# Three groups of single-column products behind the shared expert's tiles, in a four-layer kernel on one core

## The reference

```
sh = gelu(xt @ sw1 + sb1) @ sw2 + sb2
sh = sh + gelu(xt @ swd) @ swu
out = out + 0.2 * sh
```

```
xk = x * time_mix_k + (1.0 - time_mix_k) * xx
xv = x * time_mix_v + (1.0 - time_mix_v) * xx
xr = x * time_mix_r + (1.0 - time_mix_r) * xx
k = jnp.einsum('btc,oc->bto', xk, w_key)
v = jnp.einsum('btc,oc->bto', xv, w_value)
r = jax.nn.sigmoid(jnp.einsum('btc,oc->bto', xr, w_rec))
...
ww = time_first + k
```

## Time and profile before

| | us |
|---|---|
| median of 3 runs without a profile | 866.83 (865.06 to 867.51) |
| profiled execution | 858.83 |
| its span, first to last instruction | 856.3 |
| TensorE busy in it | 838.8 (98%) |

### The profile page before, as it was taken

One profiled execution on the slowest core, in us unless ns is written; L12 is line 12 of the kernel. 1 busy time (PEld: TensorE's weight loads), 2 busy tenths in 40 slices (PEclk: granted clock), 3 DMA queues, 4 the chain that ended last, 5 costly groups with the idle time before them and its releaser, 6 DMA issues.

```text
span 856.3 us, 15659 instructions
## 1 busy us (share of the span) xinstructions
PE 838.8 (98%) x5436; PEld 710.0 (83%) x5436; DVE 631.1 (74%) x1275; ACT 472.1 (55%) x944; POOL 455.6 (53%) x316
## 2 busy tenths in 40 slices
PE   8999999999999999999999999999999999999998
PEld 7888888888856899999999878778888887886688
DVE  6899999999987756655656969577667695345767
ACT  3666666676654566646643375633453425357743
POOL 6676767676614655666666021059718216708720
PEclk9999999999999999999999999999999999999999
DMA  8101010101007275456113050011111010030001
GB/s 335 39 20 37 18 37 18 37 18 37 0 1 273 87 255 202 151 185 206 63 44 96 40 209 1 0 51 50 37 37 37 13 62 1 1 148 3 3 2 50
DMA packets 23342, 62.17 MB, mean 73 GB/s; under 512 B 3136, under 2 KB 13632, under 8 KB 20224
## 3 DMA queue, kind: packets, MB, share of 16 engines
q1 hardware_dynamic: 21760, 57.35, 19.5%
q0 software_dynamic: 1536, 4.20, 1.5%
HBM read 50.00 MB, written 8.39 MB: 68 GB/s over the span
## 4 chain that ended last, share of the span: by engine, by line
PE 85%; DVE 8%; ACT 2%; POOL 2%; issue 1%; DMA 1%; SPq 0%; DVEq 0%; ACTq 0%; POOLq 0%
PE banks L102 25%; PE banks L104 24%; PE banks L103 24%; PE banks L1344 3%; DVE banks L1875 1%; PE banks L1330 1%; POOL arenaB L841 1%; POOL arenaC L841 1%; DVE arenaC_rounded L1884 1%; PE banks L999 1%; PE banks L1171 1%; PE banks L934 1%; PE banks L933 1%; PE banks L1013 1%; PE banks L854 1%
## 5 line engine op out<-in xcount | busy, mean ns | idle before, releaser
L2079 ACT ACTIVATE banks<-banks,small 128x512 f32<-128x512 f32 x128 | 84.9, 663 | 74.2 <-DVE small L1480 74.2
L1480 DVE TENSOR_REDUCE small<-banks 128x1 f32<-128x512 f32 x128 | 87.1, 680 | 4.9 <-PE banks L104 4.9
L104 PE MATMUL banks<-arenaC_rounded,arenaD_rounded 128*128 128x512 f32 (+1 forms) x256 | 89.4, 349 | 0.0
L102 PE MATMUL banks<-xnT_rounded,arenaD_rounded 128*128 128x512 f32 x224 | 88.1, 393 | 1.3 <-POOL arenaC_rounded L721 1.0
L103 PE MATMUL banks<-s_tok_rounded,arenaD_rounded 128*128 128x512 f32 x224 | 88.0, 393 | 0.0
L104 PE MATMUL banks<-xnT_rounded,arenaD_rounded 128*128 128x512 f32 x192 | 75.1, 391 | 0.0
L104 PE MATMUL banks<-xnT_rounded,arenaC_rounded 128*128 128x512 f32 x192 | 74.8, 390 | 0.0
L102 PE MATMUL banks<-arenaC_rounded 128*128 128x512 f32 (+1 forms) x192 | 70.9, 369 | 1.1 <-DVE arenaC_rounded L1633 0.6
L1495 DVE SCALAR_TENSOR_TENSOR arenaC<-banks,small,arenaC 128x512 f32<-128x512 f32 x96 | 71.4, 744 | 0.0
L103 PE MATMUL banks<-arenaD_rounded,arenaC_rounded 128*128 128x512 f32 (+1 forms) x192 | 68.0, 354 | 0.0
L707 POOL TENSOR_TENSOR arenaD_rounded<-arenaC,ones 128x512 fp32r<-128x512 f32 x30 | 31.2, 1040 | 49.6 <-DVE arenaC L1495 48.6
(11 more groups left out here) (431 smaller groups left out, 2728.8 us busy)
## 6 DMA issues: line engine op xcount, KB each, us to landing
arenaD<-in_wexp SPq DMA_DIRECT2D x8, 1060.0 KB, 6.7
arenaD<-in_wexp SPq DMA_DIRECT2D x8, 1024.0 KB, 4.9
arenaC<-in_wqkv SPq DMA_DIRECT2D x16, 384.0 KB, 3.0
arenaD<-in_wexp SPq DMA_DIRECT2D x8, 512.0 KB, 3.5
slots<-arenaB SPq DMA_DIRECT2D x1, 2560.0 KB, 10.6
arenaB<-in_sw SPq DMA_DIRECT2D x1, 2084.0 KB, 7.5
arenaC<-in_wo SPq DMA_DIRECT2D x1, 2048.0 KB, 15.5
arenaC<-slots SPq DMA_DIRECT2D x8, 256.0 KB, 3.4
```

The costliest lines, as they stand in the source:

```text
L102: pe.matmul(o, r(lhs[0]), r(rhs[0]), start=start, stop=False)
L104: return pe.matmul(o, r(lhs[1]), r(rhs[0]), start=False, stop=stop)
L1480: dve.tensor_reduce(negmax[:, n % 4:n % 4 + 1], bank[3 + n % 4][:, :], AX.X, ALU.max, negate=True).then_inc(max_done, 1)
L2079: act.activation(prob[r], prob[r], ACT.Exp, bias=negmax[:, r:r + 1], accum_out=rowsum[:, r:r + 1]).then_inc(exp_done, 1)
```

## The change

On TensorE the 24 single-column products no longer stand in one row ahead of the turns. Tile 0 of the shared expert is issued first, then the last rows' turns, and one group of eight single-column products (four in the program) follows each of tiles 1, 2 and 3, in the order key, receptance, value. Each group raises `bias_ready` by one. TensorE's waits for the weights, the vectors and `offs` stand between the turns and tile 1.

On VectorE the three small bias steps go from ahead of the tiles to behind tile 5's split and fold. `fold_rest` waits for the group whose weights it overwrites. `bias_done` now counts the scaling of `w_lin` first, then that of `sb2`, then the biases; the waits' numbers are changed accordingly. ScalarE's wait for the biases goes from ahead of its first Gelu to ahead of the second layer's first use of them, and TensorE's wait ahead of `shared_rows(0)` takes in all three counts.

```diff
@@ TensorE
-            pe.wait_ge(w1_in, 64)
-            pe.wait_ge(vec_in, 64)
-            pe.wait_ge(low_done, 1)
-            for i in range(3):
+            def mixed_bias(i):
                 for o in range(DC):
                     for c in range(DC):
                         mm = pe.matmul(bank[4][:, 2 * i + o:2 * i + o + 1], w_rwkv[:, i, c, o * P:(o + 1) * P], offs[:, i, c:c + 1],
                                        start=(c == 0), stop=(c == DC - 1))
-            mm.then_inc(bias_ready, 1)
-            rows_back(NE - 1)
+                mm.then_inc(bias_ready, 1)
...
             pe.wait_ge(w_split, 5 * NE + 2)
-            for f in range(NF + 1):
+            shared_hidden(0, 0)
+            rows_back(NE - 1)
+            pe.wait_ge(w1_in, 64)
+            pe.wait_ge(vec_in, 64)
+            pe.wait_ge(low_done, 1)
+            for f in range(1, NF + 1):
                 shared_hidden(0, f)
+                if f < 4:
+                    mixed_bias((0, 2, 1)[f - 1])
             for f in range(2):
                 shared_hidden(1, f)
-            pe.wait_ge(bias_done, 1)
+            pe.wait_ge(bias_done, 3)
@@ VectorE
-            dve.wait_ge(bias_ready, 1)
-            link(dve.tensor_copy(bias1[:, 0:3, :], bank[4][:, 0:6].rearrange("p (i c) -> p i c", i=3)))
-            link(dve.tensor_tensor(bias1[:, 0, :], bias1[:, 0, :], vec[:, 7, :], ALU.add))
-            dve.tensor_scalar(bias1[:, 3, :], bias1[:, 0, :], -1.0, None, ALU.mult).then_inc(bias_done, 1)
...
                 dve.wait_ge(fold_rounded, n + 1)
                 if n < 6:
+                    dve.wait_ge(bias_ready, n // 2 + 1)
...
                 if f < 8:
                     fold_rest(f)
+                if f == 5:
+                    link(dve.tensor_copy(bias1[:, 0:3, :], bank[4][:, 0:6].rearrange("p (i c) -> p i c", i=3)))
+                    link(dve.tensor_tensor(bias1[:, 0, :], bias1[:, 0, :], vec[:, 7, :], ALU.add))
+                    dve.tensor_scalar(bias1[:, 3, :], bias1[:, 0, :], -1.0, None, ALU.mult).then_inc(bias_done, 1)
@@ ScalarE
                 elif n == 6:
-                    act.wait_ge(bias_done, 2)
+                    act.wait_ge(bias_done, 1)
...
-            act.wait_ge(bias_done, 1)
             for b in range(B):
...
+            act.wait_ge(bias_done, 3)
             gate_silu(0, (0, 1))
```

## The result

| | before | after |
|---|---|---|
| median without a profile, same chip, 11 runs each | 863.94 (859.71 to 867.51) | 857.76 (857.46 to 858.35) |
| profiled execution | 858.83 | 857.75 |
| its span | 856.3 | 855.8 |

The ratio after to before is 0.9938, with a 95% interval of 0.9918 to 0.9958. The two profiles differ by 1.1 us (0.5 us in the span, 0.6 outside it), so they can't show where 6.2 us came from.

A forecast was written before the change was run, and what follows sets the result against it. The prediction took TensorE, busy 838.8 of 856.3 us, to bound the kernel. Clock 1.7 us, borders 0 and waits 0 turned the timed 866.83 into 865.1 us, with a range from 863.0 to 868.0.

The forecast's parts named there:

- rows: TensorE's row products behind the shared expert's tiles were to start at 455.2 us instead of 456.90.
- VectorE's splits: On VectorE, the splits were to start near 441.3 us, some 2.3 us earlier, with the bias steps moved behind them.
- The term of 1.7 us for the clock: TensorE's clock fall at 440 to 444 us was to vanish once the single-column products are spread, gaining 1.7 us.
- Rivals 1 and 2: Clock behind the thin work: falls once anyway, gain 0 (chance 0.17); or falls twice, net +1.7 us (chance 0.08).
- The rule that the prediction cites: Only long idle gaps between matmul bursts lower TensorE's clock; by it regrouping gains 0 instead of 1.7 us.
- The borders: TensorE's changes between wide tiles and single-column groups were taken to cost 0, at most 0.6 us.
- rival 3: Borders cost 0.6 us and gathers up to 0.5, leaving 0.6 of the 1.7; 866.2 us timed, chance 0.08.
- VectorE's last split of half 0: Ahead of the row products: to end by 456.4 us, needed at 458.0, a slack of 1.6 us.
- the last of the sum: The 8.0 us between timed and profiled runs of the whole kernel were carried over unchanged: 866.83 - 1.7 = 865.1 us.
- Rival 4: One more clock fall, unseen in the profile, goes with the edit: gain 3.4 us, 863.4 timed, chance 0.12.
- the prediction's own sign: Prediction wrong if rows start at 455.2 but the span isn't 1.7 us shorter: the stretch to 489.15 didn't pass it on.
- The profiled time: Whole profiled execution: 858.83 - 1.7 for the clock, borders and waits 0, giving 857.1 us.

The follow-up runs named there:

- e5: The kernel before with its 16 gathers replaced by four constant fills on GpSimd; 857.49 us.
- e6: The changed kernel with its 16 gathers replaced by four constant fills on GpSimd; 856.09 us.
- e13: The kernel before, unchanged, run again in a later set; 863.25 us (859.68 to 867.34).
- e18: The changed kernel with the 24 single-column products in two rows of 12 behind tiles 1 and 2; 865.66 us.
- e17: The changed kernel without the 24 single-column products and without VectorE's waits for them; 862.40 us.
- e3: The kernel before with only the changed places of VectorE's bias steps and ScalarE's wait, TensorE's order kept; 864.45 us.
- e8: The changed kernel with the gathers held until TensorE has finished tile 4 of half 0; 862.22 us.
- e7: The changed kernel with the row products of half 0 three tiles later, behind tile 4 of half 1; 858.29 us.

## Why the prediction was wrong

**What held.** Most local steps did. Predicted and found: turns 438.4 and 438.25; first activation near 438.7 and 438.45; first gather 443.7 and 443.54; rows 455.2 and 455.33; groups 0.86 and 0.81; VectorE's splits near 441.3 and 440.95. No engine waits on a group, and the clock is 1.00. The term of 1.7 us for the clock is right in size: e5 against e6 gives 1.4 and the runs of before 1.8. Rivals 1 and 2 are excluded. The fall stands behind products with no gap ahead, and goes when they are spread, so idle gaps alone don't explain it, as the prediction argued.

The rule that the prediction cites (the Trainium skill, "TensorE: Matmul & The Clock Gate", section "Why this matters for your kernels": no idle gaps between bursts of matmuls) fits the second fall in kind: TensorE had been busy for 0.79 and 1.02 of 2 us ahead of it, and 0.49 in the stretch in which it fell, in gaps of at most 1.51 us.

**Two small misses.** The borders were taken at 0. Three more tiles than before stand behind thin work and cost 0.1 us each, and the three groups give back 2.59 - 3 x 0.81 = 0.16 (2.59 is 439.58 - 436.99). That is inside the bound of 0.6 that rival 3 uses. VectorE's last split of half 0 was to end at 456.4 at the latest and ended at 456.87, still 1.3 us ahead of the product that reads it.

**The step that failed** is the last of the sum: "The runs without a profile have a median of 866.83 us, 8.0 above the profiled execution; no row shows where these 8 us are. I carry the difference over." It was not a property of timed against profiled runs. The profiled execution of before happened not to starve, by luck: its 100 row products took 11.79 us, what e5 takes with no gathers at all. Another execution of the same kernel, e13's profiled one, lost 7.75 us there with a second fall of the clock, and 1.2 more ahead of the rows by the longer first fall, and took 867.34. Since the changed kernel starves for about 1 us, the difference went with the edit: its profiled execution, 857.75, stands at its median, 857.76. Rival 4 looked in this direction, but it priced what comes back as one more clock fall, 1.7 us, where it was some 4.6, and the mechanism was mostly another.

One figure pointed to it beforehand: the three timed runs of before lay 6.2 to 8.7 us above the profiled execution, and 2.4 us apart. Afterwards the prediction's own sign did: the span had to become 1.7 us shorter if the rows start at 455.2. It became 0.5 shorter, and one row of the chain, the issue at 466.42, was the way in.

**The profiled time** was forecast as 857.1 and was 857.75, which is near by luck. The span became 0.5 us shorter: the rows start 1.57 us earlier, and 1.17 of that was lost in them. The other 0.6 us lie outside the span (2.53 us before, 1.95 after), and nothing forecast them.

**What stays open.** Why the order tile 0, turns, and three groups of eight puts the onset at product 84 to 94 of 100, where it comes at 21 to 69 in every other order that was profiled starving with rows and gathers at their usual place. It repeats (857.76 and 857.87 in two sets of runs, onset 86 and 94), so it belongs to the program. Short rows alone don't do it (e18), nor the lack of the products (e17), nor the clock at 1.00 early on (e3, e17, e18), and in the changed kernel the gathers' start doesn't move it (e8). Where TensorE's instructions lie was not tested in a set that starves. Nor is it known why one kernel starves in one set or execution and not in another. e5 and e6 show that the stops go with the gathers. That they end when the transfers end, and not when GpSimd is done, speaks for the transfers, but no run took one without the other.

## What to carry to other kernels

When the timed runs lie several microseconds above the profiled execution and scatter, that difference may be a cost with a place of its own, as here: profile the kernel again until a long execution is caught, before any edit is priced, and never carry the difference over as a constant. A suspected interference is priced by taking the suspect out of both kernels, as here the gathers; one part of the change at a time could not have told it. A gain that comes from how one engine's work lies against another's may go with the next edit: two rows of 12 instead of three of 8 lost all of it.

## What the runs showed of the hardware

While GpSimd's indirect gathers run, TensorE can stand with no semaphore or tile to wait for: in e13 it issued 4, 5 and 3 of the usual 19 products in two microseconds, and in 11 of 12 profiles that have such stops they ended within 0.45 us of the end of the gathers' last transfer, up to 2 us after GpSimd was done. No transfer in the queues of instructions fell into them (e13, e17). The stops met almost only the 256-column products, which want a product and a weight load every 0.118 us; at the 512-column tiles under the same gathers, 0.2277 us each, such idle time stands twice in all profiles, 0.58 us in e7 and 0.44 in e8. It differs by set of runs and by execution: on one chip the kernel before took 857.98 in a set in which none of the four profiled kernels has such a loss, and 862.67 in a later one in which four of four have it; and of its own two profiles one lost nothing and one 7.75 us. A fall of the clock behind single-column products had 1.7 us of clock missing in six profiles and 3.4 in one. 63 and 127 waits that were already met delayed TensorE's first product by 3.5 and 6.9 us, 0.055 us each, and cost 2.1 and 5.2 us in the end.
